# Splitting the sign build in two, with the layer-norm finish moved behind the value scaling, in an eight-core attention-plus-FFN kernel

## The reference

```python
xn = _layernorm(x, axis=-1)
q = l2norm((xn @ Wq) per head);  k = l2norm((xn @ Wk) per head);  v = xn @ Wv
beta = sigmoid(xn @ Wb + bb)
scores = (q @ k^T) * beta * tril          # linear attention, no softmax, 16 heads of 64
attn = (scores @ v) @ Wo
w = (weights >= 0.0) * 2.0 - 1.0          # sign of the FFN weights
ffn = clip((xn @ w^T) * scale + bias, -100, 100)
out = x + attn + ffn
```

## Time and profile before

| | us |
|---|---|
| median of 2 runs | 1052.81 (1050.82 to 1054.81) |
| the profiled execution | 1051.84 |
| its span, slowest core | 1049.6 |
| spans of the 8 cores | 1041.5 to 1049.6 |

### The profile page before, as it was taken

One profiled execution on the slowest core, in us unless ns is written; L12 is line 12 of the kernel. 1 busy time (PEld: TensorE's weight loads), 2 busy tenths in 40 slices (PEclk: granted clock), 3 DMA queues, 4 the chain that ended last, 5 costly groups with the idle time before them and its releaser, 6 DMA issues.

```text
span 1049.6 us, 14797 instructions; the slowest of 8 cores (1041.5 to 1049.6 us)
## 1 busy us (share of the span) xinstructions
PE 868.4 (83%) x5320; PEld 387.7 (37%) x5320; DVE 478.4 (46%) x900; ACT 280.5 (27%) x521; POOL 60.5 (6%) x97
## 2 busy tenths in 40 slices
PE   0009954999989989999989998999899988998995
PEld 0003322533444334433444344434443344433442
DVE  1021355533656166524655266624753365623662
ACT  0003332323231341223232333134132323134110
POOL 9100000000000000000000000000000000000000
PEclk9999965899999999999999999999999999999998
DMA  8952012050032301340033202240125003200135
GB/s 162 165 95 81 0 51 90 11 151 1 1 82 60 101 1 42 81 121 1 4 78 89 72 2 58 64 120 2 41 53 146 4 1 81 61 21 1 41 81 120
DMA packets 21126, 63.90 MB, mean 61 GB/s; under 512 B 3648, under 2 KB 3648, under 8 KB 21056
## 3 DMA queue, kind: packets, MB, share of 16 engines
q0 software_dynamic: 11840, 29.40, 16.5%
q1 hardware_dynamic: 9216, 33.56, 9.3%
HBM read 54.60 MB, written 16.78 MB: 68 GB/s over the span
## 4 chain that ended last, share of the span: by engine, by line
PE 77%; DVE 6%; DMA 5%; ACT 4%; issue 3%; POOL 3%; ACTq 1%; DVEq 0%; POOLq 0%
PE pBig L481 22%; PE pBig L811 12%; PE pBig L603 11%; PE pBig L793 10%; PE T L670 5%; DMA scale_pp<-fsc 4%; PE T L742 4%; PE T L502 3%; PE pBig L804 2%; DVE vt L631 2%; DVE sT L760 2%; DMA outt<-wf 2%; PE T L540 1%; PE T L724 1%; PE T L681 1%
## 5 line engine op out<-in xcount | busy, mean ns | idle before, releaser
L760 DVE TENSOR_TENSOR sT<-T,mask 128x512 bf16<-128x512 f32 x256 | 163.8, 683 | 133.0 <-PE T L742 133.0
L811 PE MATMUL pBig<-signT,xnT 128*128 128x512 bf16 x512 | 127.6, 394 | 0.0
L793 PE MATMUL pBig<-Wo,ctxT 128*128 128x512 bf16 x512 | 126.1, 391 | 0.0
L481 PE MATMUL pBig<-xnT,Wq 128*128 128x512 bf16 x512 | 123.0, 384 | 1.4 <-ACT xnT L455 1.4
L481 PE MATMUL pBig<-xnT,Wk 128*128 128x512 bf16 x512 | 120.2, 380 | 0.0
L603 PE MATMUL pBig<-Wv,xnT 128*128 128x512 bf16 x512 | 111.9, 379 | 0.0
L731 ACT COPY fb<-T 128x512 f32<-128x512 f32 x64 | 38.4, 600 | 264.6 <-PE T L724 263.9
L670 PE MATMUL T<-sT,vt 128*64 128x256 bf16 x512 | 65.3, 299 | 29.7 <-DVE sT L760 25.2
L449 PE MATMUL T<-ident,xn_nat 128*128 128x128 bf16 x256 | 19.0, 232 | 79.8 <-DVE xn_nat L437 77.9
L494 DVE TENSOR_TENSOR sT<-qT 128x512 bf16<-128x512 bf16 x64 | 27.2, 425 | 108.0 <-ACT qT L489 55.7
L837 POOL DMA_DIRECT2D outt<-x x32 | 27.7, 864 | 835.7 <-DVE outt L828 835.7
(11 more groups left out here) (79 smaller groups left out, 776.6 us busy)
## 6 DMA issues: line engine op xcount, KB each, us to landing
xf<-x SPq DMA_DIRECT2D x32, 512.0 KB, 6.9
outt<-x POOLq DMA_DIRECT2D x32, 512.0 KB, 5.5
out<-outt SPq DMA_DIRECT2D x32, 512.0 KB, 2.7
outt<-wf POOLq DMA_DIRECT2D x8, 512.0 KB, 4.0
Wq<-wq POOLq DMA_DIRECT2D x8, 256.0 KB, 11.1
Wk<-wk POOLq DMA_DIRECT2D x8, 256.0 KB, 23.7
Wv<-wv POOLq DMA_DIRECT2D x8, 256.0 KB, 32.1
Wo<-wo POOLq DMA_DIRECT2D x8, 256.0 KB, 36.5
```

The costliest lines, as they stand in the source:

```text
L481: (lambda wname, dt_, di, pb, sp: lambda e: e.matmul(ps[pb][:, :], w_slice(wname, di, dt_ * 128, (dt_ + 1) * 128), sb["xnT"][:, (sp * NT + ...
L760: (lambda h01, st_base, gsc=gscs[h01]: lambda e: e.tensor_tensor(sb["sT"][:, (st_base + h01 * 2) * CK:(st_base + h01 * 2 + 2) * CK], ps[gs ...
L793: (lambda cs_, pt, lt, dc, pw: lambda e: e.matmul(ps[pw][:, :], sb["ctxT"][:, (cs_ * (H // 2) + pt) * CK + lt * 128: (cs_ * (H // 2) + pt) ...
L811: (lambda di, dc, span_lt, pyp, sp: lambda e: e.matmul(ps[pyp][:, :], sb["xnT"][:, (sp * NT + di) * SPAN + span_lt * 128: (sp * NT + di) * ...
```

## The change

The sign build is cut in two. `emit_sign_dve` holds the load and the two VectorE operations, `emit_sign_pe` the transposes and the evacuations. The loads alternate between the second and third quarter of `outt`, with a semaphore each, and the result alternates between `sgn_buf` and half of the fourth quarter of `outt`. The first two tiles are loaded and signed during the value projection of the first span, ahead of jobs 6 and 7; from then on each head pair of the first chunk issues the transposes of its tile and then the load and the VectorE work of the tile two further on. `emit_ln_finish` is taken out of the value projection in every span and is called after the eight products that scale v, ahead of the first chunk.

```diff
-    cs_wf = P.new_sem("cwf")
+    cs_wf = [P.new_sem("cwf0"), P.new_sem("cwf1")]
...
-    def emit_sign_ot(ot):
+    sgn_slot = [sb["sgn_bf"], sb["outt"][:, 3 * D:3 * D + 512].bitcast(BF16)]
+    sgn_res = ["sgn_buf", "outt.3.0"]
+
+    def emit_sign_dve(ot):
+        r = 1 + (ot % 2)
+        s = ot % 2
         P.dma("gpsimd",
...
+                  sb["outt"][:, r * D:(r + 1) * D], wf_hbm[ot * 128:(ot + 1) * 128, :]))(ot, r),
+              cs_wf[ot % 2], writes=[f"outt.{r}.0", f"outt.{r}.1"], tag=f"wf{ot}")
...
+             reads=[f"outt.{r}.0", f"outt.{r}.1"], writes=[sgn_res[s]], tag=f"sgn{ot}")
...
+             reads=[sgn_res[s], f"scale_pp.{ot}", "scale2_pp"],
+             writes=[sgn_res[s]], tag=f"sgs{ot}")
+
+    def emit_sign_pe(ot):
+        s = ot % 2
         g = new_gen()
...
+                 reads=[sgn_res[s], "ident"], writes=[g], tag=f"str{ot}.{ib}")
...
+    sgn_dve = [(lambda ot: lambda: emit_sign_dve(ot))(_ot) for _ot in range(NT)]
+
     def pop_D(n=1):
         for _ in range(n):
             if pending_D[0]:
                 pending_D[0].pop(0)()
+            if sgn_dve:
+                sgn_dve.pop(0)()
...
-        pending_D[0].append((lambda ot: lambda: emit_sign_ot(ot))(_ot))
+        pending_D[0].append((lambda ot: lambda: emit_sign_pe(ot))(_ot))
...
-                if i == 6 and pending_lnfin is not None:
-                    emit_ln_finish(*pending_lnfin)
+                if i in (6, 7) and gspan == 0 and sgn_dve:
+                    sgn_dve.pop(0)()
...
                          writes=[f"vt.{lt}.{dc}"], tag=f"vfold{lt}.{dc}")
+
+            if pending_lnfin is not None:
+                emit_ln_finish(*pending_lnfin)
```

More of the change, by code:

```diff
@@ L331, in build_program @@
          reads=[f"scale_pp.{t}" for t in range(NT)], writes=["scale2_pp"], tag="sc2")
-    def emit_sign_ot(ot):
+    sgn_slot = [sb["sgn_bf"], sb["outt"][:, 3 * D:3 * D + 512].bitcast(BF16)]
[3 more added lines that the diff above has]
+        s = ot % 2
         P.dma("gpsimd",
-              (lambda ot: lambda e: e.dma_start(sb["wf_f32"][:, :], wf_hbm[ot * 128:(ot + 1) * 128, :]))(ot),
-              cs_wf, writes=["outt.0.0", "outt.0.1"], tag=f"wf{ot}")
+              (lambda ot, r: lambda e: e.dma_start(
+                  sb["outt"][:, r * D:(r + 1) * D], wf_hbm[ot * 128:(ot + 1) * 128, :]))(ot, r),
+              cs_wf[ot % 2], writes=[f"outt.{r}.0", f"outt.{r}.1"], tag=f"wf{ot}")
         P.op("vector",
-             (lambda ot: lambda e: e.tensor_scalar(sb["sgn_bf"][:, :], sb["wf_f32"][:, :],
-                                                   0.0, None, ALU.is_ge))(ot),
-             reads=["outt.0.0", "outt.0.1"], writes=["sgn_buf"], tag=f"sgn{ot}")
+             (lambda ot, r, s: lambda e: e.tensor_scalar(
+                 sgn_slot[s][:, :], sb["outt"][:, r * D:(r + 1) * D],
+                 0.0, None, ALU.is_ge))(ot, r, s),
+             reads=[f"outt.{r}.0", f"outt.{r}.1"], writes=[sgn_res[s]], tag=f"sgn{ot}")
         P.op("vector",
[L342 to L347, removed]
+             (lambda ot, s: lambda e: e.tensor_scalar(
+                 sgn_slot[s][:, :], sgn_slot[s][:, :],
+                 sb["scale2_pp"][:, ot:ot + 1],
+                 sb["scale_pp"][:, ot:ot + 1],
+                 ALU.mult, ALU.subtract))(ot, s),
+             reads=[sgn_res[s], f"scale_pp.{ot}", "scale2_pp"],
+             writes=[sgn_res[s]], tag=f"sgs{ot}")
+    def emit_sign_pe(ot):
+        s = ot % 2
         g = new_gen()
@@ L350, in emit_sign_ot @@
             P.op("tensor",
-                 (lambda ot, ib, g: lambda e: e.transpose(
+                 (lambda ot, ib, g, s: lambda e: e.transpose(
                      tv_bf(g, ib),
-                     sb["sgn_bf"][:, ib * 128:(ib + 1) * 128], sb["ident"][:]))(ot, ib, g),
-                 reads=["sgn_buf", "ident"], writes=[g], tag=f"str{ot}.{ib}")
+                     sgn_slot[s][:, ib * 128:(ib + 1) * 128], sb["ident"][:]))(ot, ib, g, s),
+                 reads=[sgn_res[s], "ident"], writes=[g], tag=f"str{ot}.{ib}")
         for ib in range(NT):
```

## The result

The changed kernel takes 1064.14 us (median of 12 runs) against 1051.31 (10 runs): a ratio of 1.0111, 95% interval 1.0092 to 1.013. It is slower by about 1%. Its profiled execution took 1060.64 us, with a span of 1058.0 on the slowest core, core 3, against 1049.6 before.

What follows compares the result with a forecast made beforehand. TensorE, busy 83%, was taken as the main bound, with load round trips binding the first chunk and VectorE's queue the span starts. Finish +25.2 less sign build 14.5 gave +10.7 us, said as 1063; range 1055 to 1075.

Steps and rivals of the forecast that it cites:

- The first chunk: First span's first chunk: the split sign build ends it 14.5 us earlier, the finish included; bounds 12 to 17.
- the step on their timing: First-chunk weight loads: issued two pairs ahead, landing in 4.0 us, each is early enough with just over 1 us to spare.
- The period of 3.2 us: First chunk: VectorE bounds the six pairs that still sign a tile, at 3.2 us per pair, 19.2 us in all.
- The finish: Spans 2 to 7, between scaling of v and first masked evacuation: delays by 4.2 us per span, 25.2 us in all.
- The half microsecond: Behind the moved finish: TensorE's scores and projection end about 281, VectorE's evacuation 281.3, so the delay is VectorE's.
- The sign named for it: Spans 2 to 7, behind the scaling of v: TensorE's wait there grows over 4 us beyond 1.93.
- The clock terms: Start of each span's first chunk: projection about 1.5 us slower, three quarters exposed; FFN matmuls might regain 1.0; taken to cancel.
- The high end of the forecast: Whole kernel: finish costing 5.5 us per span if the clock loses, 33 - 14.5 = +18.5 us.
- Rival A: Span starts: clock stays low until the FFN matmuls are through, 7.5 us per span, +30 us, 1083; chance 0.14.
- Rival B: Span starts: the finish's delay is absorbed, only the sign build counts, 1052.8 - 14.5 = 1038; chance 0.08.
- Rival C: First chunk: loads still bind at 6.9 us landing, 4.05 a pair, 5 us lost, 1068; chance 0.06.
- Rival D: Start-up: the second early load delays it by up to 2.5 us, 1066; chance 0.06.

Runs made afterwards that it cites:

- e1: Kernel before with only the sign build split, the layer-norm finish left in the value projection: 1033.34 us, ratio 0.9825.
- e7: Changed kernel with 24 unused filler matmuls in TensorE's standstill behind the transposes of k, spans 2 to 8: 1055.17 us, ratio 1.001 to the kernel before.
- e4: Kernel before with epsilon, Ln and Exp moved behind the scaling of v, mean and tiles threaded into head pairs 2 to 5: ratio 1.0265.
- e2: Kernel before with only the layer-norm finish moved behind the scaling of v, sign build as before: 1084.58 us, ratio 1.0315.
- e6: e1 with both load buffers made one, so each load waits for the compare of the tile before: 1045.55 us, ratio 0.992 to the kernel before.
- e10: Changed kernel with the layer-norm finish emitted behind the evacuations of k: ratio 1.0067 to the kernel before.
- e3: Kernel before with only the four xn_nat tiles of the finish moved behind the scaling of v: ratio 1.0267.
- e9: e8 with deferred v-scaling products singly in pairs 1, 2, 5, 6 and the transposes behind odd pairs: 993.6 us, ratio 0.943 to the kernel before.
- e8: e5 with the next span's layer-norm transposes spread over pairs 2 to 5 of the second chunk: 1017.46 us, ratio 0.9645 to the kernel before.
- e5: e1 with four of eight v-scaling products moved into pairs 5 and 7 of the first chunk: 1024.78 us, ratio 0.972 to the kernel before.

## Why the prediction was right, and where only its number was

**The sum.** +10.7 us was forecast on the profiled execution, 1051.84 to 1062.5; it went to 1060.64, +8.8. The predicted 1063 stands against a median of 1064.14. That it came so close is in part luck: the first chunk gained 2.0 us more than was said, the finish cost 1.8 more in spans 2 to 7, and these two errors cancel. The rest of the difference lies in the table's other rows.

**The first chunk** was to gain 14.5 us and gained 16.5. The loads left the chain, as the step on their timing had it, but with less to spare than the "just over 1 us": the six that were issued in the chunk or in the value projection took 4.1 to 5.6 us to land, where 4.0 was taken, and one was waited for. VectorE was taken as the bound. It was busy for 14.49 of 16.20 us in the signing pairs and TensorE, at clock 0.50, for 14.29, and the chain of waits runs mostly through TensorE's work; neither is shown to be the bound alone. The period of 3.2 us was taken for all six signing pairs. The trace has 2.4 for the first, which has no `ctxT` product yet, 3.0 to 3.4 for those that follow, and 2.3 to 2.8 at the end, where the loop of transposes and copies had been given 3.4 in one pair. e1 measures the split without the finish at 18 us where the terms gave 14.5 + 4.2 = 18.7. The reading of the kernel before was too simple as well. Its chain holds four loads and not seven. In the other three pairs the compare did not wait for its load, and the chain runs through the signing, the transposes, the copies and the context of one and the same pair, a loop that the split also opens.

**The finish** was to cost 25.2 us in six spans and cost 27.0 between the scaling and the second broadcast. The size was right and the path was not. The prediction worked out both arrivals and gave the delay to VectorE, since they lay within half a microsecond "if the clock stays high". It did not stay high. In all six spans the k evacuations, held up behind Ln, and the projection at 3.6 us made TensorE the later one, by 1.5 us (context at +11.38 against +9.84 in e7). e4 shows that this path alone, without the tiles, gives the same +11.38. The half microsecond was the failed step: a tie between two paths was broken on a clock that the delay itself lowers. The sign named for it failed with it: TensorE's wait ahead of the first context did not grow by over 4 us but went to nothing, and 5.93 us stand ahead of the scores instead. With the clock held high, in e7, the step is right: the context waits 0.51 us for VectorE, and the six spans lose 25.0 us by the estimate given there.

**The clock terms** were left to cancel, and by the same estimate did so within 2 us: 1.5 us on the projection, three quarters exposed, against 1.0 gained on the FFN group in five of six spans (five on the slowest core, two to four on the others). The trace has both, 3.60 for 1.90 and 1.90 for 2.8 to 3.0. Two spans lost more: the fourth 5.9 us, with projection and FFN group both low (3.60 and 3.59), and the sixth 5.5, the span in which the kernel before had paid nothing. The Trainium skill, "TensorE: Matmul & The Clock Gate", section "What's actually happening", has the throttled clock as the default and activity as what releases it. e7 agrees: 5.3 us of useless activity in each standstill made the kernel 10 us faster. The high end of the forecast, +18.5 us, was too high all the same, because the same clock had already been paid for before the change, one group later.

**Rival A** (clock low through the FFN group, 7.5 us a span) did not come: the FFN group was at 1.90 in five of six spans. It came nearest in the fourth span, with 5.9. **Rival B** (absorbed) is refuted by e2 at +33 us. **Rival C** (loads still bind) was near: one compare on the slowest core idles 0.55 us behind its load, and the largest landing time was 5.6 us, between the 4.0 of the forecast and the 6.9 of the rival; e6 shows what it looks like when they bind. **Rival D** (later start-up): `scale_pp` is ready at 68.5 to 71.7 us on the eight cores before and at 69.2 to 71.4 after, so no delay; the 1.9 us in the table's first row is that the slowest core is another one, for the first scaling starts at 137.9 to 141.7 on the eight cores before and at 137.0 to 140.2 after.

**Left open:** e2 costs 33 us, of which the stretches from the scaling to the second broadcast hold 28 in seven spans, less 1.6 in the eighth, and 2 are a later start, so that some 4 are not placed; and whether e10's 4 us below the changed kernel are a gain, since the two profiled executions are equal. In its trace the six stretches from the scaling to the second broadcast are 4.0 us longer than in the changed kernel, and those from there to the next scaling 4.5 us shorter.

## What to carry to other kernels

A wait put into an in-order queue costs whatever stands behind it: 0.2 us of VectorE and two small ScalarE operations ahead of the k evacuations cost as much as 3 us of tiles (e4, e3). Before a piece is moved, look in each queue that it touches, not only its main one, for what the busiest engine will need next, and put the piece where that engine has a backlog. Spread singly, deferred products cost little: in e9, with one product each in pairs 1 and 2, the second to the third broadcast takes 6.75 us against 6.15 in e8. In a lump ahead of the last pair they brought a wait of 2.40 us and a slow group behind it (e5). Parts of one change should be timed apart: here one part gained 18 us and the other lost 33.

## What the runs showed of the hardware

- In these traces a TensorE standstill of 5.0 to 5.9 us (in e10 two, of 2.76 and 2.89 us) is followed by some microseconds at the 1.2 GHz level, and the cost falls on a group behind it: the projection (3.60 instead of 1.90 us) in the changed kernel, the FFN group (3.59) in e3 and e10. Moving the work does not avoid it; filling the standstill (e7) or removing it (e9) does.
- Useless matmuls can make a kernel faster: 37 us of work added by e7, 10 us of time gained.
- With two loads of 512 KB under way, the six of the changed kernel's first chunk and value projection took 4.1 to 5.6 us from issue to landing; one at a time, in the kernel before, the seven of the first chunk took 3.8 to 4.2.
